# Attention mask and a routed feed-forward layer: four staging places for expert weights, casts moved behind another copy, and one-hots of all pairs kept at once

## The reference, cut to what matters

```python
# x (4, 512, 512), ctx_512 (4, 512, 128): four sequences of 512 tokens
def attn(ctx, h):                      # h = layernorm(x), used as the "adjacency"
    Q, K = ctx @ Wq.T, ctx @ Wk.T
    sim = Q @ K.T / (sqrt(32) * 4)     # 512 x 512 for each sequence (sum over the heads)
    thr = top_k(sim, 153)[..., -1:]
    A = sigmoid(sim) * (sim >= thr)
    A = (A + A.T) * 0.5
    return (1 - gamma) * h + gamma * A
x = x + attn(ctx_512, layernorm(x))

def ffn(x):                            # x = layernorm(x), 2048 tokens of 512
    probs = softmax(x @ router_w.T)    # 8 experts
    w, idx = top_k(probs, 2)           # two experts for each token
    w = w / sum(w)
    moe = sum over the two experts e of w_e * ((silu(x @ gate[e]) * (x @ up[e])) @ down[e])   # 352 wide
    shared = (silu(x @ s_gate + b) * (x @ s_up + b)) @ s_down + b                             # 704 wide
    return moe + shared
x = x + ffn(layernorm(x))
```

## Time and profile before

| | us |
|---|---|
| three runs | 641.94, 643.76, 650.61 |
| median | 643.76 |
| the profiled execution, its time | 645.95 |
| its span, first to last instruction | 644.0 |
| TensorE busy | 507.6 (79%) |
| VectorE, ScalarE, GpSimd busy | 351.0, 244.7, 189.5 |

### The profile page before, as it was taken

One profiled execution on the slowest core, in us unless ns is written; L12 is line 12 of the kernel. 1 busy time (PEld: TensorE's weight loads), 2 busy tenths in 40 slices (PEclk: granted clock), 3 DMA queues, 4 the chain that ended last, 5 costly groups with the idle time before them and its releaser, 6 DMA issues.

```text
span 644.0 us, 9811 instructions
## 1 busy us (share of the span) xinstructions
PE 507.6 (79%) x2994; PEld 277.0 (43%) x2995; DVE 351.0 (55%) x1003; ACT 244.7 (38%) x433; POOL 189.5 (29%) x245
## 2 busy tenths in 40 slices
PE   5120569959895989598995968899988989999971
PEld 2000334424442454244463545455545545666640
DVE  1798878687768867872774333334344434222220
ACT  3643364435635274414522223344433334122210
POOL 0021250005100230015034614334443333444441
PEclk9755759979997999889996978899999999999996
DMA  6501240006400370016121755576666665353441
GB/s 185 167 17 33 82 148 2 0 9 145 127 1 1 86 177 0 0 67 132 47 61 56 168 141 143 119 160 164 143 153 167 143 153 137 67 96 69 96 78 23
DMA packets 36417, 60.54 MB, mean 94 GB/s; under 512 B 5641, under 2 KB 16137, under 8 KB 36370
## 3 DMA queue, kind: packets, MB, share of 16 engines
q0 software_dynamic: 10384, 23.34, 20.6%
q1 hardware_dynamic: 25986, 36.60, 18.1%
HBM read 37.64 MB, written 22.28 MB: 93 GB/s over the span
## 4 chain that ended last, share of the span: by engine, by line
PE 47%; DVE 21%; DMA 11%; issue 9%; ACT 7%; SPq 3%; POOL 2%; DVEq 0%; POOLq 0%; ACTq 0%
PE bank L901 6%; PE bank L903 6%; PE bank L902 6%; DMA stage<-L_ffn_up_w_in 6%; DMA stage<-L_ffn_down_w_in 4%; DVE W L1091 4%; PE bank L916 3%; PE bank L917 2%; PE bank L918 2%; SPq L384 2%; DVE xT L1395 2%; PE bank L847 2%; ACT hS L780 2%; DVE stats L1114 2%; PE bank L1039 2%
## 5 line engine op out<-in xcount | busy, mean ns | idle before, releaser
L1406 DVE TENSOR_TENSOR hS<-bank,hS 128x384 f16<-128x384 f32 x35 | 19.5, 557 | 126.6 <-ACT hS L780 126.6
L901 PE MATMUL bank<-xT,W 128*128 128x512 f16 x192 | 73.9, 385 | 0.0
L903 PE MATMUL bank<-xT,W 128*128 128x512 f16 x192 | 73.8, 384 | 0.0
L902 PE MATMUL bank<-xT,W 128*128 128x512 f16 x192 | 73.8, 384 | 0.0
L540 POOL DMA_INDIRECT out_dram<-xb,sidx x35 | 56.3, 1607 | 30.0 <-POOL sidx L539 27.8
L588 ACT ACTIVATE W<-stage 128x704 f16<-128x704 f32 (+1 forms) x62 | 43.5, 708 | 48.8 <-DMA stage<-L_ffn_up_w_in 29.0
L1037 PE MATMUL bank<-W,hS 128*128 x105 | 41.4, 395 | 11.1 <-DVE hS L1406 11.1
L788 ACT ACTIVATE xb<-bank,wcol 128x512 f32<-128x512 f32 x35 | 24.0, 687 | 68.6 <-PE bank L1039 68.6
L1091 DVE SCALAR_TENSOR_TENSOR W<-stage,W 128x704 f16<-128x704 f32 (+1 forms) x49 | 37.3, 793 | 14.5 <-ACT W L588 14.5
L1013 PE MATMUL bank<-W,xT 128*128 x140 | 44.3, 316 | 0.4 <-issue 0.3
L470 POOL TENSOR_TENSOR rstd<-pw 128x4 f32<-128x4 f32 x12 | 13.0, 1083 | 106.0 <-DVE pw L1119 106.0
(11 more groups left out here) (228 smaller groups left out, 1071.7 us busy)
## 6 DMA issues: line engine op xcount, KB each, us to landing
stage<-L_ffn_down_w_in SPq DMA_DIRECT2D x24, 256.0 KB, 2.9
stage<-L_ffn_gate_w_in SPq DMA_DIRECT2D x32, 176.0 KB, 2.5
stage<-L_ffn_up_w_in SPq DMA_DIRECT2D x32, 176.0 KB, 2.9
xn_dram<-xn SPq DMA_DIRECT2D x17, 256.0 KB, 2.1
xb<-x_in SPq DMA_DIRECT2D x4, 1024.0 KB, 6.3
out_dram<-xb SPq DMA_DIRECT2D x16, 256.0 KB, 2.1
out_dram<-ysh POOLq DMA_DIRECT2D x12, 256.0 KB, 4.3
stage<-L_ffn_s_down_w_in SPq DMA_DIRECT2D x6, 256.0 KB, 2.8
```

Source lines behind the costliest of these rows:

```text
L901: pe.matmul(o, wh, xT[:, 0, c, :], start=(c == 0), stop=False)
L902: pe.matmul(o, wh, xT[:, 1, c, :], start=False, stop=False)
L903: last = pe.matmul(o, wl, xT[:, 0, c, :], start=False, stop=(c == KD - 1))
```

## The change

Three things. (1) From the first ranked expert on there are four staging places (`place_of`): two in `stage` as before and two in `sim`; a load waits for the unit four before it. (2) One-hots and values of all 32 groups are kept at once, in the slots of `W` for the fourth and fifth expert, in rounds of 8 groups with no wait for the table's matmuls; the table's last 16 groups are multiplied behind hidden slice 5, ahead of output tile 0. (3) ScalarE casts more of the units early (`FIRST_AT`, `SECOND_AT`), in a block between `routed_h` and `routed_sig`, and two fewer blocks carry units.

```diff
-HEAD_BLOCKS = 23
-RING = 8
-GROUP = 4
-TABLE_AT = {3: (0, 8), 4: (8, 16), 5: (16, 24), SC: (24, 2 * NT)}
+HEAD_BLOCKS = 21
+GROUP = 8
+TABLE_AT = {3: (0, 8), 4: (8, 16), 5: (16, 2 * NT)}
+PLACES = 4
-FIRST_AT = [0, 0, 2, 1, 1, 2, 1]
-SECOND_AT = [0, 1, 1, 1]
+FIRST_AT = [0, 0, 3, 2, 1, 1, 0]
+SECOND_AT = [2, 2, 2, 1]
+def place_of(n):
+    return n % 2 if n < RANKED else (n - RANKED) % PLACES
@@ staged
-        return stage[:, n % 2, 0:cols], d_stage[n % 2]
+        place = place_of(n)
+        if place < 2:
+            return stage[:, place, 0:cols], d_stage[place]
+        return simf[:, (place - 2) * SI:(place - 2) * SI + cols], d_stage[place]
@@ memory of the one-hots
-    oneh = simf[:, 0:RING * P].rearrange("p (a b) -> p a b", a=RING)
-    valh = simf[:, RING * P:RING * (P + 2 * BLOCKS)].rearrange("p (a k b) -> p a k b", a=RING, k=2)
+    oneh = W[:, 3 * EW:3 * EW + 4 * NT * P].bitcast(F32).rearrange("p (a b) -> p a b", a=2 * NT)
+    marks = W[:, 4 * EW:4 * EW + 12 * NT * BLOCKS].bitcast(F32)
+    valh = marks[:, 0:4 * NT * BLOCKS].rearrange("p (a k b) -> p a k b", a=2 * NT, k=2)
@@ SyncE, load_ranked
-            if n - 2 < SECOND:
-                sp.wait_ge(s_wlo, n - 2 - EARLY + 1)
+            last = n - PLACES
+            if last < RANKED:
+                sp.wait_ge(s_wlo, SC)
+            elif last < SECOND:
+                sp.wait_ge(s_wlo, last - EARLY + 1)
             else:
-                sp.wait_ge(s_wloD, EARLY + n - 2 - SECOND + 1)
+                sp.wait_ge(s_wloD, EARLY + last - SECOND + 1)
@@ ScalarE, step
-        split_some(BLOCK_UNITS)
...
                 routed_h(j - 1, 1 - p)
+            if isinstance(j, int) and j < HEAD_BLOCKS:
+                split_some(BLOCK_UNITS)
             routed_sig(j, p)
             if not first_block:
                 routed_y(j - 1, m if p else m - 1, 1 - p)
-            if isinstance(j, int) and j + 1 < HEAD_BLOCKS:
-                split_some(BLOCK_UNITS)
@@ TensorE
         shared_down(NB - 1, 0)
-        table(*TABLE_AT[SC])
         shared_down(NB - 1, 1)
@@ VectorE, one_hots
-            at, half = GROUP * q, GROUP * (q % 2)
-            if q >= 2:
-                dve.wait_ge(s_tabp, at - GROUP)
+            at = slice(GROUP * q, GROUP * (q + 1))
...
-        one_hots(1)
...
             if q < SC - 1:
-                one_hots(2 * q - 2)
-                one_hots(2 * q - 1)
+                one_hots(q - 1)
@@ VectorE, ahead of the blocks
-        later_weights(2)
+        later_weights(4)
         routed_x(0, 0)
-        later_weights(sum(SECOND_AT) - 2)
+        later_weights(sum(SECOND_AT) - 4)
```

More of the change, by code:

```diff
@@ L99 @@
 assert all(sum(SECOND_AT) + BLOCK_UNITS * min(4 * r - 1, HEAD_BLOCKS) >= PER_EXPERT * r for r in range(1, E))
+def place_of(n):
+    return n % 2 if n < RANKED else (n - RANKED) % PLACES
 def stage_counts():
-    at, early, out = [0, 0], [0] * 4, []
+    at, early, out = [0] * PLACES, [0] * 4, []
     for n, (src, *_) in enumerate(UNITS):
@@ L109, in stage_counts @@
         else:
-            at[n % 2] += 16 * len(src)
-            out.append(at[n % 2])
+            at[place_of(n)] += 16 * len(src)
+            out.append(at[place_of(n)])
     return out
@@ L186, in build @@
     simf = sim[:, :, :].rearrange("p a b -> p (a b)")
[L187 to L189 removed]
+    oneh = W[:, 3 * EW:3 * EW + 4 * NT * P].bitcast(F32).rearrange("p (a b) -> p a b", a=2 * NT)
+    marks = W[:, 4 * EW:4 * EW + 12 * NT * BLOCKS].bitcast(F32)
+    valh = marks[:, 0:4 * NT * BLOCKS].rearrange("p (a k b) -> p a k b", a=2 * NT, k=2)
+    eqh = marks[:, 4 * NT * BLOCKS:6 * NT * BLOCKS].rearrange("p (a b) -> p a b", a=2 * NT)
     xg = [t[:, :].bitcast(F16) for t in (qT, kT)]
@@ L262, in build @@
     d_y = [sem(f"d_y{i}") for i in range(2)]
-    d_stage = [sem(f"d_stage{i}") for i in range(2)]
+    d_stage = [sem(f"d_stage{i}") for i in range(PLACES)]
     d_xg = [sem(f"d_xg{i}") for i in range(2)]
@@ L452, in split_lo @@
             src, hi, lo, cols, zero = UNITS[n]
-            st = stage[:, n % 2, 0:cols]
+            st = staged(n)[0]
             pool.wait_ge(s_whi, n - EARLY + 1)
@@ L941, in table @@
                     pe.wait_ge(s_lgc, NB)
-                pe.matmul(bank[0][:, 0:2 * BLOCKS], oneh[:, n % RING, :],
-                          valh[:, n % RING, :, :].rearrange("p k b -> p (k b)"),
+                pe.matmul(bank[0][:, 0:2 * BLOCKS], oneh[:, n, :],
+                          valh[:, n, :, :].rearrange("p k b -> p (k b)"),
                           start=(n == 0), stop=(n == 2 * NT - 1)).then_inc(s_tabp, 1)
@@ L1349, in one_hots @@
         def one_hots(q):
-            at, half = GROUP * q, GROUP * (q % 2)
-            if q >= 2:
-                dve.wait_ge(s_tabp, at - GROUP)
+            at = slice(GROUP * q, GROUP * (q + 1))
             def over(row, m):
-                return row[:, at:at + GROUP].rearrange("p (n o) -> p n o", o=1).to_broadcast([P, GROUP, m])
+                return row[:, at].rearrange("p (n o) -> p n o", o=1).to_broadcast([P, GROUP, m])
             def each(row, m):
                 return row[:, 0:m].rearrange("p (o b) -> p o b", o=1).to_broadcast([P, GROUP, m])
[L1361 to L1364, removed]
+            link(dve.tensor_tensor(eqh[:, at, :], each(iota, BLOCKS), over(higf, BLOCKS), ALU.is_equal))
+            dve.tensor_tensor(oneh[:, at, :], each(iota, P), over(lowf, P), ALU.is_equal)
+            dve.tensor_tensor(valh[:, at, 0, :], eqh[:, at, :], over(tokn, BLOCKS), ALU.mult)
+            dve.tensor_tensor(valh[:, at, 1, :], eqh[:, at, :], over(wtn, BLOCKS), ALU.mult).then_inc(s_oneh, 1)
         shared_hidden(last_b, 1)
```

## The result

The changed kernel takes 602.83 us (median of four runs, 600.93 to 604.22) against 644.88 us of the kernel before, a ratio of 0.934 (95% interval 0.929 to 0.938): 42 us less. The forecast was 602. The profiled execution has a span of 599.7 us against 644.0.

A forecast was written before the change was run, and what follows sets the result against it. TensorE sets 6.30 us a block; late weight loads add 1.34, and an idle stretch precedes tile 0. Gains 9.35 + 3.5 + 2.4 + 29.4 = 44.7 us, less 2.5: 42 off 643.76 gives 602 us, range 597 to 616.

The forecast's parts named there:

- one-hots and table, to tile 1: Ahead of tile 0: TensorE's idle stretch goes, full clock, tile 1 begins at 344.50 instead of 353.85; gain 9.35 us.
- block 0's wait for a load: Block 0: ScalarE's 3.72 us wait of a cast for its load goes; gain 3.5 us.
- interval of block 0 to 1: From block 0's SiLU to block 1's: 5.8 us at the full clock instead of 8.16; gain 2.4 us.
- blocks 1 to 23: Blocks with casts: loads issued about two blocks ahead, 22 intervals of 6.30 us instead of 7.64; gain 29.4 us.
- taken off for denser transfers: Transfers around and in the blocks with casts: busier DMA engines make some block lose a microsecond; 2.5 us deducted.
- all that lies ahead of 306 us: Code before the changed front: everything ahead of 301 us keeps its order; 0 us.
- the third: Ahead of tile 0: idle stretch stays as collisions use up the slack and casts delay a SiLU; 611 us, chance 0.09.
- the fifth: In the blocks: late loads ahead of the SiLU delay everything behind it, making it slower; 663 us, chance 0.03.
- cost 0 on the casts' new position: In the blocks: casts ahead of the SiLU are covered by the 24 up matmuls; cost 0, 2 us to spare.
- Slack of the one-hots: VectorE before the last hidden slice: 2 us of slack, with up to 1.3 us more a round where GpSimd collides.
- The second: In the blocks: transfers are the next bound, each scatter waiting for the last one's landing; 608 to 614 us, chance 0.20.
- The fourth: In the blocks: loads stay late, intervals stay at 7.64 us, only the front is gained; 632 us, chance 0.06.

The follow-up runs named there:

- two places: The changed kernel with two staging places instead of four and the first expert's early casts counted as in the kernel before; 619.77 us, ratio 0.961.
- front only: The kernel before with only the one-hots of all pairs and the table ahead of tile 0 as changed; 636.85 us, ratio 0.989.
- position only: The kernel before with one edit, a block's two casts moved behind the copy of the hidden rows, ahead of the SiLU; 618.41 us, ratio 0.960.

## Why the prediction was right, and where it was not

**The sum.** By its own steps, against the two profiled executions:

| step | forecast | measured |
|---|---|---|
| one-hots and table, to tile 1 | 9.35 | 353.85 - 343.87 = 9.98, less 1.36 = 8.6 |
| block 0's wait for a load | 3.5 | 13.67 - 9.98 = 3.7 |
| interval of block 0 to 1 | 2.4 | 8.16 - 6.14 = 2.0 |
| blocks 1 to 23 | 29.4 | 168.04 - 139.17 = 28.9 |
| taken off for denser transfers | -2.5 | -0.3 behind block 23, none before |
| all that lies ahead of 306 us | 0 | 1.4 |
| span | 42 | 44.3 |

The 1.36 us are those by which the last sequence's first hidden product on VectorE comes earlier (305.90 against 307.26), where the code did not change; I take them for the difference of two executions. That is not shown: in all ten traces with the one-hots in `W` this product starts at 304.55 to 306.35, in the two with the one-hots in `sim` at 307.26 and 310.64, so some of it may belong to the change. Every gain lies within 1 us of its forecast, and the deduction of 2.5 us for denser transfers, the one wrong term, did not come: the two traces are 44.3 us apart, near the bare sum of 44.7. That the medians differ by 42.05, as forecast with the deduction, is luck: the profiled executions (645.95 and 601.87 us) differ by 44.1, one of them 1.1 us above and the other 1.0 us below its median. Two sums among the rivals are off by a little: the third starts from 604, the number against the profiled run, where the forecast's 602 gives 609 to 611, and the fifth's 663 comes to 662 from its own terms (599 + 21 x 3).

**Place and position.** This is the step that was right in its number and incomplete in its reason. I put the 29.4 us on the number of places and cost 0 on the casts' new position. Zero holds with four places (602.11 against 602.83). But with two places the same move brings 1.1 of the 1.34 us an interval. Both give the load time before it hurts, and either is nearly enough (6.54 us an interval by the position alone, 6.36 by four places alone, of 7.64): the position turns its wait into one under 24 matmuls of TensorE; two more places issue it a block earlier. The prediction's sentence that with two places a load can be issued only when the unit two before it has been split holds for either order. What it leaves out is what is queued behind the waiting cast: before, the copy of the hidden rows, for which TensorE's down product waits; in the new order the SiLU, which cannot start before the up product ends. What the places bring on top of the position shows in "two places" mostly ahead of the blocks, where ScalarE needs seven units behind four tiles: of the 21.8 us between the profiled spans (621.5 and 599.7; the medians differ by 16.9) 12.3 are lost before block 0's SiLU, 2.3 in the next interval and 6.8 in the twenty after it. How much of this is the counts' and not the places' was not measured. A kernel with the front, the new position, two places and the old counts was not run; adding up the gains of "front only" and "position only" (7.3 and 24.6 us) puts it at about 612 us, an estimate, which would leave some 10 us to the places and the counts made for them.

**Slack of the one-hots.** I allowed one collision of up to 1.3 us a round; rounds 1 to 3 lost 1.9, 3.0 and 2.2 us, and the low parts between them up to 1.3. The 2 us of slack that I gave the last hidden slice shrank to less than nothing, and TensorE waited 0.52 us. The rule of the Trainium skill ("SBUF — State Buffer", "Who interferes with whom") was borne out by the run with GpSimd held back. My price for it was too small; the second half of the table, which TensorE did meanwhile, covered all but the 0.52 us.

**The rivals.** The second is refuted as a bound at this load and shown as a mechanism: the scatter's cycle is 5.0 + 1.0 = 6.0 us of the 6.30 at the median landing, GpSimd waits 17 times for landings between 362 and 490, and TensorE never for a gather in that stretch:

```profile
POOL sidx L551 <- DMA out_dram<-xb,sidx: 28.1, 17, 3.0
```

With 57% more bytes of weights it does: 6.71 us an interval. That this is near the 6.7 that I had put at the worst landing is chance, as it is a mean of intervals of 6.3 and of 7 to 8 us and not a steady 6.7. The third (idle stretch stays) was right only for 0.5 us. The fourth is refuted by the intervals. The fifth, a late load ahead of the SiLU costing more than behind the output copy, is refuted where it would have had to show: "position only" has late loads ahead of the SiLU (23.1 us of waits) and is 25 us faster. The landings of 12 us and more from which the prediction let it decide occur in no trace.

## What to carry to other kernels

Before adding buffers for a late load, look at what the waiting instruction stands in front of: moving a wait to where another engine has several microseconds of work of its own may bring most of the gain, and the buffers the rest. When two engines pass a small memory to and fro in pieces, the reader's place in its own order sets the writer's pace; memory that will be used only later can hold all pieces at once. After such a step look for the next chain by its cycle against the pace: here a scatter that waits for its predecessor's landing fills 6.0 of 6.3 us, and in the blocks it was the first to break when loads were added.

## What the runs showed that I had not expected

GpSimd's two-step split stretches VectorE's instructions much beyond one collision: the 312-element product, 0.48 us alone, took 1.04 to 1.79 us in rounds 1 and 2, and a round of 2.5 us as much as 5.5. And the changed kernel's GpSimd runs permanently late, behind its scatters' landing (26.5 us of waits from 384 to 487), while with the casts behind the output and the same loads it waits only 2.2 us for landings in that stretch; both run at TensorE's pace. Why the lag, once there, is not made up in the one and does not arise in the other was not settled.
